# Block-count prefix of a token ranking: 31 TensorE products replaced by one VectorE scan of 512

## The chip, the cores and the metric

One Trainium2 chip, one of its cores. The metric is the device time of the whole program in microseconds (us), as a median over several executions. Lines are named L1, L2, ... after the line of the kernel before. The engines are PE (TensorE), DVE (VectorE), ACT (ScalarE), POOL (GpSimd) and SP (the DMA-issuing queue).

## The reference, cut to what matters

The input is layer-normalised and goes through two branches whose outputs are added to it: an attention with relative-position bias (16 heads, 4 x 512 tokens) and a block whose q, k, v and output maps are hard-routed binary trees of depth 8. Each of the 2048 tokens walks one tree down to one of 256 leaves and uses that leaf's own small two-layer network:

```python
def _fff(x, nw, nb, w1, b1, w2, b2, act):
    node = jnp.zeros(x.shape[:2], dtype=jnp.int32)
    for _ in range(DEPTH):
        logit = jnp.einsum('bsd,bsd->bs', x, nw[node]) + nb[node]
        node = 2 * node + 1 + (logit > 0).astype(jnp.int32)
    leaf = node - NN
    h = act(jnp.einsum('bsd,bsdl->bsl', x, w1[leaf]) + b1[leaf])
    return jnp.einsum('bsl,bsld->bsd', h, w2[leaf]) + b2[leaf]
```

There are four trees: q, k and v on the normalised input, and f on the attention's output.

## The kernel before, in words

Tokens stand as 16 tiles of 128 (NT = 16, P = 128). Eight neighbouring leaves make one block, so there are 32 blocks (BLK = 32). For each tree the kernel sorts the tokens by block: every token gets a slot in a padded list in which each block begins at a multiple of 128, POOL scatters the token rows to their slots in HBM, and the tree's network then runs on 48 tiles of the list in 12 groups of four, with one block's weights per tile.

The slot of a token is: the padded start of its block, plus the number of tokens of that block in earlier tiles, plus the number in earlier partitions of its own tile. `ranks` (L1023 to L1035, PE) and `ranked` (L613 to L638, DVE) compute it from a one-hot table `o` of 16 tiles x 32 blocks (512 columns, bf16).

- `ranks` waits for the one-hot (semaphore oh5). Into the PSUM bank rank[0] it puts one product with a strictly triangular matrix, which counts earlier partitions of the same tile (L1029), and 15 products with a matrix of ones: tile i's counts are broadcast over all later tiles, 480, 448, ... 32 columns wide (L1031). Into rank[1] it adds up 16 products of 32 columns, the total of every block (L1034). The last one raises rk.
- `ranked` waits for rk. It rounds the totals up to 128 (L618 to L620), makes a prefix over the 32 blocks by a scan (L622 to L625), adds it to rank[0] over 512 columns (L627, raises rt), multiplies by the one-hot and sums (L631, L632), writes the slots (L633, raises sl, for which POOL's scatter waits), and finds each list tile's block (L635 to L637, raises id). `then` makes an instruction raise a counter and DVE wait for it before the next one.

This runs four times. For q, k and v it lies in the opening stretch, one loop over 12 pieces i (three trees, four pieces each) on PE, DVE and ACT. On PE, piece i issues `logits(i)` (L994), at c = 2 `ranks` of the tree before, then `follow(i-1)` (L1005) and `settled(i-2)` (L1018). `settled` of a tree's first piece writes the banks that `ranked` reads, and so waits for rt. On DVE, piece i issues `bits_of(i)` (L645), at c = 1 `places` (L652 to L657, raises oh5), at c = 2 `ranked` to its end. ACT runs L845 on `follow`'s result, and later sends a small DMA per tree once id is raised (`tile_blocks`, L836).

After that PE does the v products (L1063), projections (`project`, L1070 to L1073) and the main loop: 16 steps of 20 slots, written out by hand. In a slot PE computes one 128 x 512 tile of scores twice (`scores_q`, L1084, for the row maximum, and `scores_k`, L1095 and L1097, for the exponential), DVE takes the maximum (`row_max`, L693), ACT the exponential (L873), and PE weighs values (L1107). `max_rows` (L1122) transposes the maxima after a step's last `row_max`, `sub_max` (L699) subtracts them, and the next step's `scores_k` waits for it. The stages of the trees' networks (L1155, L1161, L1166, L1171 on PE) are fitted into fixed slots.

The f tree's routing is fitted in too. `route_y` on PE issues `ranks` in slot 188. On DVE a generator, `route_f`, is advanced once per slot, behind that slot's `row_max`, from slot 174 on; each `yield` ends a slot's share. `ranked` falls into slots 196 (L618 to L620), 197 (L622 to L627) and 198 (L631 to L637); slot 199 is the last of its step. The f tree's network starts in slot 226.

Of the kernel before, what the change touches and what calls it, by code (L numbers as in the profile page):

```python
# [24 lines left out]
ALU = mybir.AluOpType  # L25
# [3 lines left out]
P = 128  # L29
NB, NS = 4, 512  # L30
KT = NS // P
NT = NB * KT
# [10 lines left out]
BLK = LEAVES // LB  # L43
# [73 lines left out]
def build(nc, x, wq, wk, wv, wp, bp, table, onehot, cf, cb, nw, nb, wl, b2, out):  # L117
# [7 lines left out]
    with ctx:  # L125
        def sb(name, shape, dt=F32):
            return ctx.enter_context(nc.sbuf_tensor(name, shape, dt))
# [50 lines left out]
        whole = sb("whole", [P, BLK], I32)  # L178
# [28 lines left out]
        ps = ctx.enter_context(nc.psum_tensor("ps", [P, 8, NS], F32))  # L207
# [5 lines left out]
        bank = lambda i: ps[:, i, :]  # L213

        S = {n: ctx.enter_context(nc.semaphore(n)) for n in (
            "d_ew0 d_ew1 d_ew2 d_ew3 d_x d_c d_w d_u d_b d_f d_z d_n d_sc tc pa oh hb pop z_mx pl tab_in d_far aug lkc mxc "
            "sl tick rt_in rt_out ones ln_m ln_r ln_sub ln_sq ln_out xT_ps xT_sb xnT_sb tab_ps tab_sb v_ps v_sb lg bit oh5 rk rt id wsc "
            "proj p1 mt p2 pv ot at pr h ex osb ats vr qs ks km max qs2 rc norm acc "
            "lx0 lx1 lw0 lw1 st xT xTs hh hr mk hm yy yl d_nf yT_ps yT_sb "
            "g_y g_v0 g_v1 g_v2 g_v3 g_b g_o0 g_o1 g_o2 g_o3 t_ps t_sb s_ps s_mx s_ex pT_ps pT_sb o_ps y_sb y_add dv d_out").split()}  # L220
# [261 lines left out]
        def _(dve):  # L482
            V = nc.vector
            count = [0]

            def then(ins):

                count[0] += 1
                ins.then_inc(S["dv"], 1)
                dve.wait_ge(S["dv"], count[0])  # L490
# [122 lines left out]
            def ranked(t, work, rank):  # L613

                here = work.bitcast(BF16)[:, 30 * NT:62 * NT].rearrange("p (t n) -> p t n", n=BLK)
                dve.wait_ge(S["rk"], t + 1)
                c = lambda i, n=BLK: sm[:, i, 0:n]
                then(V.tensor_scalar(whole[:], ps[:, rank[1], 0:BLK], float(P - 1), None, ALU.add))  # L618
                then(V.tensor_scalar(whole[:], whole[:], -P, None, ALU.bitwise_and))
                then(V.tensor_copy(c(0), whole[:]))  # L620
                yield
                V.memset(c(2), 1.0)  # L622
                then(V.memset(c(3), 0.0))
                then(V.tensor_tensor_scan(c(3), c(2), c(0), 0.0, ALU.mult, ALU.add))
                then(V.tensor_tensor(c(1), c(3), c(0), ALU.subtract))  # L625
                rows = work[:, 32 * NT:64 * NT].rearrange("p (t n) -> p t n", n=BLK)
                V.tensor_tensor(rows, bank(rank[0]).rearrange("p (t n) -> p t n", n=BLK),  # L627
                                c(1).unsqueeze(1).to_broadcast([P, NT, BLK]), ALU.add).then_inc(S["rt"], 1)
                dve.wait_ge(S["rt"], t + 1)
                yield  # L630
                then(V.tensor_tensor(rows, rows, here, ALU.mult))  # L631
                then(V.tensor_reduce(st[:, 5, :], rows, X, ALU.add))  # L632
                V.tensor_copy(slot[:, t, :], st[:, 5, :]).then_inc(S["sl"], 1)  # L633

                then(V.tensor_scalar(c(2), c(3), col(C_T), None, ALU.is_le))  # L635
                then(V.tensor_reduce(sm[:, 4, 0:1], c(2), X, ALU.add))
                then(V.tensor_scalar(ewc[:, t:t + 1], sm[:, 4, 0:1], float(BLK - 1), float(BLK * t), ALU.min, ALU.add))  # L637
                dve.sem_inc(S["id"], 1)  # L638
# [24 lines left out]
            for i in range(NTREE * CHUNKS + 3):  # L663
                if i < NTREE * CHUNKS:
                    bits_of(i)
                t, c = divmod(i, CHUNKS)
                if c == 1 and t > 0:
                    places(t - 1, t1)
                if c == 2 and t > 0:
                    for _ in ranked(t - 1, t1, (0, 1)):  # L670
                        pass
# [60 lines left out]
            def route_y():  # L732

                for k in range(4):
                    dve.wait_ge(S["yT_ps"], k + 1)
                    V.tensor_copy(yT[:, k * NS:(k + 1) * NS], bank(FB[k % 2])).then_inc(S["yT_sb"], 1)
                    if k % 2:
                        yield
                dve.wait_ge(S["d_nf"], 32)
                then(V.tensor_scalar(nb_f, nb_f, -1.0, None, ALU.mult))  # L740
                yield
                yield from decide(TF, nb_f, bits_f.bitcast(BF16)[:, 0:NT * NODES].rearrange("p (t n) -> p t n", n=NODES), work_f,
                                  [(k, FB[k % 2]) for k in range(8)])
                yield from ranked(TF, work_f, FB)
# [216 lines left out]
        def _(pe):  # L961
            T = nc.tensor
# [5 lines left out]
            for i, t in enumerate((xTs, hr)):  # L968
                b_ = WB - 1 + i
                last = T.matmul(ps[0:H, b_, :], tab_s, flat(t[0:BUCKETS]), start=True, stop=True)  # L970
# [52 lines left out]
            def ranks(t, work, rank):  # L1023

                wb = work.bitcast(BF16)
                o = wb[:, 30 * NT:62 * NT].rearrange("p (t n) -> p t n", n=BLK)
                tri, ones = cbt[:, 0], cbt[:, 1]
                pe.wait_ge(S["oh5"], t + 1)
                T.matmul(bank(rank[0]), tri, wb[:, 30 * NT:62 * NT], start=True, stop=False)  # L1029
                for i in range(NT - 1):  # L1030
                    T.matmul(ps[:, rank[0], (i + 1) * BLK:], ones, o[:, i:i + 1, :].to_broadcast([P, NT - 1 - i, BLK]),  # L1031
                             start=False, stop=i == NT - 2)
                for i in range(NT):
                    last = T.matmul(ps[:, rank[1], 0:BLK], ones, o[:, i, :], start=i == 0, stop=i == NT - 1)  # L1034
                last.then_inc(S["rk"], 1)  # L1035

            pe.wait_ge(S["xnT_sb"], 4)
# [3 lines left out]
            for h in range(2):  # L1041
                for k in range(2):
                    last = T.matmul(ps[:, PATH_BANKS[0], h:h + 1], paths[:, k, h * P:(h + 1) * P], cbt[:, 1, 0:1],
                                    start=k == 0, stop=k == 1)
            n = 2 * (NTREE + 1)
            T.transpose(ps[:, PATH_BANKS[0], 2:2 + n], nb_rows, cst[0:n, C_ID:C_ID + n]).then_inc(S["pop"], 1)
            pe.wait_ge(S["pop"], 2)
            for i in range(NTREE * CHUNKS + 3):
                if i < NTREE * CHUNKS:
                    logits(i)  # L1050
                t, c = divmod(i, CHUNKS)
                if c == 2 and t > 0:
                    ranks(t - 1, t1, (0, 1))
                if 1 <= i <= NTREE * CHUNKS:
                    follow(i - 1)
                if 2 <= i <= NTREE * CHUNKS + 1:
                    settled(i - 2)
# [3 lines left out]
            for k in range(4):  # L1061
                for i in range(4):
                    last = T.matmul(quarter(VB[k], i), xnT[:, (4 * k + i) * P:(4 * k + i + 1) * P], wv_s[:], start=True, stop=True)  # L1063
# [168 lines left out]
            def route_y(after):  # L1232

                for k in {0: (0, 1), 1: (2, 3)}.get(after, ()):
                    y_transposed(k)
                for k in {3: (0, 1), 4: (2,), 5: (3,), 6: (4,), 7: (5,), 8: (6,), 9: (7,)}.get(after, ()):
                    y_logits(k)
                if after == 14:
                    ranks(TF, work_f, FB)
# [130 lines left out]
```

## Time and profile before

| | us |
|---|---|
| median of 3 runs | 673.77 (671.25 to 674.9) |
| the profiled execution, its own time | 670.35 |
| its span in the trace | 668.3 |
| PE busy | 581.6 |
| DVE busy | 414.0 |
| ACT busy | 354.4 |
| POOL busy | 274.7 |

The profiled execution's own time is 2.05 us over its span, and 3.42 us under the median of the runs. Busy time counts instructions at work; idle time in brackets in a timeline is that of the engine just before the instruction, with what ended it. PEclk is the granted TensorE clock: 1.00 is 2.4 GHz, 0.50 is 1.2 GHz.

### The profile page before, as it was taken

What the parts mean: (1) busy time and instruction counts of PE and PEld (TensorE: products, weight loads), DVE (VectorE), ACT (ScalarE), POOL (GpSimd) and SP (SyncE); (2) the same over time, 40 slices, a digit from 0 to 9 for tenths busy, and PEclk for the clock granted to TensorE, in tenths of its full rate; (3) what the DMA queues carried; (4) which work ended last, traced back from release to release, by engine and by line L of the source; (5) the groups of instructions that cost most, each with busy time, mean ns of one, the idle gap of its engine ahead of it and who ended that gap; (6) DMA issues with size and microseconds to landing.
All of it is one profiled execution on the core that took longest, in us unless ns stands there. A gap on an engine that the chain in (4) does not pass through costs nothing.

```text
span 668.3 us, 11751 instructions
## 1 busy us (share of the span) xinstructions
PE 581.6 (87%) x3641; PEld 408.9 (61%) x3641; DVE 414.0 (62%) x967; ACT 354.4 (53%) x762; POOL 274.7 (41%) x288
## 2 busy tenths in 40 slices
PE   2289868999999999999999999988698989988976
PEld 0144457777777777777775656755265667675643
DVE  3856657666666666576766665576867564756730
ACT  4633323655556565555655546423244877786533
POOL 7951776770357870760038300000077800000880
PEclk9889998999999999999999999998789999999988
DMA  7988756785668794886512200000033654542231
GB/s 224 266 170 206 259 144 170 214 218 157 184 192 217 177 210 129 185 193 166 151 41 36 37 0 1 1 1 0 1 111 69 116 135 127 144 122 69 31 49 47
DMA packets 108701, 83.05 MB, mean 124 GB/s; under 512 B 8680, under 2 KB 105840, under 8 KB 108640
## 3 DMA queue, kind: packets, MB, share of 16 engines
q1 hardware_dynamic: 93344, 69.68, 38.8%
q0 software_dynamic: 15104, 12.63, 10.3%
q8 instruction: 29, 0.48, 0.3%
q14 instruction: 32, 0.26, 0.1%
q10 hardware_dynamic: 192, 0.00, 0.0%
HBM read 57.91 MB, written 24.36 MB: 123 GB/s over the span
## 4 chain that ended last, share of the span: by engine, by line
PE 62%; DVE 8%; ACT 8%; issue 5%; SPq 1%; DMA 0%; DVEq 0%; ACTq 0%
PE ps L1095 8%; PE ps L1107 8%; PE ps L1097 8%; PE ps L1084 7%; PE ps L1171 6%; PE ps L1161 6%; PE ps L1070 3%; DVE ps L693 3%; PE ps L1214 2%; PE ps L1228 2%; ACT hr L884 2%; ACT L873 2%; PE ps L1155 2%; PE ps L1166 2%; ACT L884 2%
## 5 line engine op out<-in xcount | busy, mean ns | idle before, releaser
L693 DVE CUSTOM_DVE_ANT_0 ps<-ps,strip 128x512 f32<-128x512 f32 x256 | 177.5, 699 | 110.9 <-PE ps L1084 105.2
L873 ACT ACTIVATE pt<-ps 128x512 f32<-128x512 f32 x256 | 150.6, 600 | 99.0 <-PE ps L1097 96.5
L1095 PE MATMUL ps<-qs,km 128*128 128x512 f32 x256 | 128.4, 501 | 8.7 <-ACT pt L873 7.4
L1084 PE MATMUL ps<-km,qs 128*128 128x512 f32 x256 | 112.1, 442 | 10.9 <-DVE mx L693 7.0
L432 POOL DMA_INDIRECT yt<-ys,slot x48 | 74.5, 1552 | 80.7 <-DMA ys<-yl 66.7
L884 ACT ACTIVATE hr<-ps,wt 128x128 f32<-128x128 f32 x192 | 54.9, 368 | 66.7 <-PE ps L1161 66.6
L1097 PE MATMUL ps<-u_lo,rev_r 128*128 128x220 f32 (+1 forms) x256 | 75.3, 294 | 0.0
L1097 PE MATMUL ps<-u_hi,rev_r 128*128 128x220 f32 (+1 forms) x256 | 73.8, 288 | 0.0
L1095 PEld LDWEIGHTS ps<-qs,km 128*128 128x128 f32 x256 | 49.6, 194 | 34.9 <-ACT pt L873 21.4
L427 POOL DMA_INDIRECT xs<-xr,slot x64 | 62.5, 977 | 19.7 <-issue 18.3
L1107 PE MATMUL ps<-pt,v_aug 128*32 128x512 f32 x512 | 69.9, 619 | 0.7 <-ACT pt L873 0.7
L425 POOL CAST xr<-part_of 128x16 f32<-128x16 int32 x4 | 0.9, 213 | 156.9 <-DVE slot L633 130.4
L1161 PEld LDWEIGHTS ps<-xTs,wt 128*128 128x128 f32 x384 | 48.3, 194 | 24.6 <-issue 21.7
L1084 PEld LDWEIGHTS ps<-km,qs 128*128 128x128 f32 x256 | 49.5, 194 | 21.7 <-DVE mx L693 13.8
L432 POOL DMA_INDIRECT xr<-ys,slot x16 | 25.1, 1571 | 86.9 <-DMA ys<-yl 82.4
L1097 PEld LDWEIGHTS ps<-u_lo,rev_r 128*128 128x128 f32 x256 | 49.1, 192 | 11.4
L1161 PE MATMUL ps<-xTs,wt 128*128 128x128 f32 x384 | 54.5, 286 | 1.7 <-DMA wt<-in_wl 1.7
L432 POOL DMA_INDIRECT yt<-in_b,leaf x48 | 45.8, 954 | 20.6 <-issue 14.0
L1097 PEld LDWEIGHTS ps<-u_hi,rev_r 128*128 128x128 f32 x256 | 50.0, 195 | 5.1 <-issue 4.1
L1171 PE MATMUL ps<-wt,hm 128*128 128x128 f32 x384 | 52.4, 280 | 0.7
L1171 PEld LDWEIGHTS ps<-wt,hm 128*128 128x128 f32 x384 | 49.8, 194 | 4.5 <-DVE hm L725 3.1
L725 DVE SCALAR_TENSOR_TENSOR hm<-ps,cst,hr 128x512 f32<-128x512 f32 x48 | 36.0, 749 | 17.7 <-ACT hr L884 11.5
(227 smaller groups left out, 898.0 us busy)
## 6 DMA issues: line engine op xcount, KB each, us to landing
wt<-in_wl SPq DMA_DIRECT2D x192, 128.5 KB, 2.3
xl<-xs SPq DMA_DIRECT2D x48, 258.0 KB, 3.6
ys<-yl SPq DMA_DIRECT2D x48, 256.0 KB
xs<-mx SPq DMA_DIRECT2D x2, 3096.0 KB, 21.6
strip<-bias_bf SPq DMA_DIRECT2D x1, 3584.0 KB, 37.1
u_hi<-bias_hi SPq DMA_DIRECT2D x1, 2496.0 KB, 15.7
u_lo<-bias_lo SPq DMA_DIRECT2D x1, 2496.0 KB, 28.1
xs<-xr,slot POOLq DMA_INDIRECT x64
```

The source lines that it names most:

```text
L427: pool.indirect_dma_start(out=xs[t % 2][:, :], out_offset=bass.IndirectOffsetOnAxis(ap=slot[:, t, k:k + 1], axis=0), in_=xr[:, k, :], in_o ...
L432: pool.indirect_dma_start(out=dst, out_offset=None, in_=src[:, :], in_offset=bass.IndirectOffsetOnAxis(ap=idx, axis=0), compute_op=op).the ...
L693: V.tensor_tensor_reduce(out=bank(u % 2), in0=bank(u % 2), in1=strip[:, HG * g + j, b0:b0 + NS], scale=1.0, scalar=LOWEST, op0=ALU.add, op ...
L725: V.scalar_tensor_tensor(flat(hm[:]), bank(BB[k]), col(C_LEAF), flat(hr[:]), ALU.is_equal, ALU.mult).then_inc(S["hm"], 1)
L873: A.activation(pt[:, kt % 2, j, :], bank(2 + u % 2), ACT.Exp).then_inc(S["ex"], 1)
L884: last = A.activation(hr[:, i, :], ps[:, BB[k], i * P:(i + 1) * P], ACT.Relu if n < NTREE * GROUPS else ACT.Gelu, bias=wt[:, par, i, 2 * P ...
L1084: T.matmul(bank(u % 2), qs[:, par, qt * P:(qt + 1) * P], backward(km[:, par, j, :]), start=True, stop=True).then_inc(S["p1"], 1)
L1095: T.matmul(bank(2 + u % 2), km[:, par, j, kt * P:(kt + 1) * P], qs[:, par, :], start=True, stop=False)
L1097: last = T.matmul(ps[:, 2 + u % 2, lo:hi], rev_r[:], half[:, HG * g + j, u0:u0 + hi - lo], start=False, stop=stop)
L1107: last = T.matmul(ps[HR * j:HR * j + HR, OB, :], v_aug[:, par, kt, j, :], pt[:, kt % 2, j, :], start=kt == 0, stop=kt == KT - 1)
L1161: last = T.matmul(quarter(BB[k], i), wt[:, par, i, 0:P], xTs[:, i, :], start=True, stop=True)
L1171: last = T.matmul(quarter(BB[k], i), hm[:, i, :], wt[:, par, i, P:2 * P], start=True, stop=True)
```

## The change

`ranks` keeps the triangular product and replaces the 15 + 16 others by one product with the matrix of ones over all 512 columns, read block by block (moving operand with tiles innermost), so that rank[1] holds every tile's count of every block, ordered block, tile. `ranked` makes one running sum over these 512 counts, into `run` (513 columns of `work`, the first of them zero). The difference of the sums at a block's end and its beginning is the block's total; the running sum before a tile, less the sum at the block's beginning, is the number of tokens in earlier tiles. So `c(1)` is lessened by the sums at the blocks' beginnings, and `rows` takes a second addition of 512 columns, of `starts`, read with the two axes exchanged. A `yield` is added between the two additions, and rt is raised by the second. One memset (of `c(3)`) goes, one (of the first column of `run`) comes, and `whole` is made from `c(0)` in SBUF.

```diff
-                then(V.tensor_scalar(whole[:], ps[:, rank[1], 0:BLK], float(P - 1), None, ALU.add))
+                run = work[:, 64 * NT:96 * NT + 1]
+                starts = run[:, 0:32 * NT].rearrange("p (n t) -> p n t", t=NT)
+                V.memset(run[:, 0:1], 0.0)
+                then(V.memset(c(2), 1.0))
+                then(V.tensor_tensor_scan(run[:, 1:32 * NT + 1], c(2)[:, 0:1].to_broadcast([P, 32 * NT]),
+                                          bank(rank[1]), 0.0, ALU.mult, ALU.add))
+                then(V.tensor_tensor(c(0), run[:, 1:32 * NT + 1].rearrange("p (n t) -> p n t", t=NT)[:, :, NT - 1], starts[:, :, 0],
+                                     ALU.subtract))
+                then(V.tensor_scalar(whole[:], c(0), float(P - 1), None, ALU.add))
                 then(V.tensor_scalar(whole[:], whole[:], -P, None, ALU.bitwise_and))
                 then(V.tensor_copy(c(0), whole[:]))
                 yield
-                V.memset(c(2), 1.0)
-                then(V.memset(c(3), 0.0))
                 then(V.tensor_tensor_scan(c(3), c(2), c(0), 0.0, ALU.mult, ALU.add))
                 then(V.tensor_tensor(c(1), c(3), c(0), ALU.subtract))
+                then(V.tensor_tensor(c(1), c(1), starts[:, :, 0], ALU.subtract))
                 rows = work[:, 32 * NT:64 * NT].rearrange("p (t n) -> p t n", n=BLK)
-                V.tensor_tensor(rows, bank(rank[0]).rearrange("p (t n) -> p t n", n=BLK),
-                                c(1).unsqueeze(1).to_broadcast([P, NT, BLK]), ALU.add).then_inc(S["rt"], 1)
+                then(V.tensor_tensor(rows, bank(rank[0]).rearrange("p (t n) -> p t n", n=BLK),
+                                     c(1).unsqueeze(1).to_broadcast([P, NT, BLK]), ALU.add))
+                yield
+                V.tensor_tensor(rows, rows, starts.rearrange("p n t -> p t n"), ALU.add).then_inc(S["rt"], 1)
                 dve.wait_ge(S["rt"], t + 1)
...
             def ranks(t, work, rank):
 
                 wb = work.bitcast(BF16)
-                o = wb[:, 30 * NT:62 * NT].rearrange("p (t n) -> p t n", n=BLK)
                 tri, ones = cbt[:, 0], cbt[:, 1]
                 pe.wait_ge(S["oh5"], t + 1)
-                T.matmul(bank(rank[0]), tri, wb[:, 30 * NT:62 * NT], start=True, stop=False)
-                for i in range(NT - 1):
-                    T.matmul(ps[:, rank[0], (i + 1) * BLK:], ones, o[:, i:i + 1, :].to_broadcast([P, NT - 1 - i, BLK]),
-                             start=False, stop=i == NT - 2)
-                for i in range(NT):
-                    last = T.matmul(ps[:, rank[1], 0:BLK], ones, o[:, i, :], start=i == 0, stop=i == NT - 1)
+                T.matmul(bank(rank[0]), tri, wb[:, 30 * NT:62 * NT], start=True, stop=True)
+                by_block = wb[:, 30 * NT:62 * NT].rearrange("p (t n) -> p n t", n=BLK)
+                last = T.matmul(bank(rank[1]), ones, by_block, start=True, stop=True)
                 last.then_inc(S["rk"], 1)
```

## Rows read from the trace of the kernel before

**Rows 1.** The page, part 4: shares of the chain that ended last.

```profile
PE 62%; DVE 8%; ACT 8%; issue 5%; SPq 1%; DMA 0%; DVEq 0%; ACTq 0%
```

**Rows 2.** Busy time by stretches: from:to, length, busy by engine, PEclk, DMA share, GB/s.

```profile
64.70:72.70 8.00, 8.00 (x48) 3.86 (x47) 5.43 (x10) 3.80 (x6) 6.18 (x7) 1.00 0.99 363
```

**Rows 3.** Timeline, first ranking: start, length, engine, line, operation, count, idle before.

```profile
57.39 1.43 DVE L645 TENSOR_SCALAR yt<-ps,nbT 128x512 bf16<-128x512 f32 x2
...
57.87 0.38 PE L1029 MATMUL ps<-pt,cbt 128*128 128x512 bf16 x1
...
58.09 1.80 PE L1031 MATMUL ps<-pt,cbt 128*128 128x480 bf16 x15
...
60.14 1.02 PE L1005 MATMUL ps<-yt,b_pT 128*128 128x512 bf16 x4
60.33 0.19 DVE L618 TENSOR_SCALAR whole<-ps 128x32 int32<-128x32 f32 x1 [1.50 <-PE ps L1034]
...
61.44 0.19 DVE L625 TENSOR_TENSOR sm<-sm 128x32 f32<-128x32 f32 x1
61.67 0.69 DVE L627 TENSOR_TENSOR pt<-ps,sm 128x512 f32<-128x512 f32 x1
...
62.51 0.35 PE L1018 MATMUL ps<-b_pT,yt 128*128 128x33 bf16 x8 [1.35 <-DVE pt L627]
...
64.72 1.41 DVE L645 TENSOR_SCALAR yt<-ps,nbT 128x512 bf16<-128x512 f32 x2
```

**Rows 4.** Timeline, third ranking and the start of the main loop.

```profile
87.57 0.19 DVE L618 TENSOR_SCALAR whole<-ps 128x32 int32<-128x32 f32 x1 [2.34 <-PE ps L1034]
...
91.16 1.28 ACTq L836 DMA_DIRECT2D ew<-ewc  x2
...
91.80 1.12 PE L1070 MATMUL ps<-xnT,wk_s 128*128 128x512 f32 x2 [0.69 <-ACT v_all L849]
...
93.32 0.60 ACT L861 ACTIVATE ks<-ps 128x512 fp32r<-128x512 f32 x1 [1.57 <-PE ps L1073]
...
97.34 0.80 PE L1084 MATMUL ps<-km,qs 128*128 128x512 f32 x1 [3.34 <-DVE qs L676]
```

**Rows 5.** Timeline, the f tree's ranking in the main loop and after it.

```profile
461.01 0.39 PE L1029 MATMUL ps<-yt,cbt 128*128 128x512 bf16 x1 [2.06 <-DVEq L591]
...
463.95 0.77 PE L1095 MATMUL ps<-qs,km 128*128 128x512 f32 x1
...
465.85 0.70 DVE L693 CUSTOM_DVE_ANT_0 ps<-ps,strip 128x512 f32<-128x512 f32 x1 [3.15 <-PE ps L1084]
...
482.73 0.69 DVE L631 TENSOR_TENSOR yt<-yt 128x512 f32<-128x512 f32 x1
...
485.20 0.70 DVE L693 CUSTOM_DVE_ANT_0 ps<-ps,strip 128x512 f32<-128x512 f32 x1 [0.30 <-DVE ewc L637]
...
486.01 1.06 PE L1122 MATMUL ps<-cst,mx 128*128 128x128 f32 x4 [3.40 <-DVE mx L693]
...
487.11 0.69 DVE L699 TENSOR_TENSOR qs<-qs,ps 128x512 fp32r<-128x512 f32 x1 [1.16 <-PE ps L1122]
...
488.65 0.99 PE L1095 MATMUL ps<-qs,km 128*128 128x512 f32 x1
...
506.69 16.72 SPq L266 DMA_DIRECT2D xl<-xs  x3
...
518.77 0.66 PE L1155 MATMUL ps<-cst,xl 128*128 128x128 f32 x4
```

**Rows 6.** Groups by form on DVE: line, shapes, count, busy us, mean ns, idle.

```profile
L631 DVE TENSOR_TENSOR pt<-pt 128x512 f32<-128x512 f32 x3 | 2.1, 692 | 0.1
...
L624 DVE TENSOR_TENSOR_SCAN sm<-sm 128x32 f32<-128x32 f32 x4 | 0.9, 225 | 0.1
```

**Rows 7.** Busy time in two stretches at the lower clock (columns as in Rows 2).

```profile
462.40:465.40 3.00, 3.00 (x30) 2.68 (x29) 0.30 (x1) 0.12 (x1) 0.00 (x0) 0.50 0.00 0
97.00:103.60 6.60, 6.26 (x23) 5.17 (x24) 3.57 (x10) 1.74 (x5) 5.02 (x6) 0.50 0.29 89
```

## Prediction, made before the changed kernel was run

> **What bounds the kernel now.** I read the chain that ended last first: TensorE holds 62% of it and VectorE 8% [rows 1], so on the whole an instruction saved on PE is worth something and one added on DVE little. But the ranking lies at four places, and each has a bound of its own, so the timelines decide. In the opening stretch PE and DVE take turns around a ranking: DVE finishes `bits_of` at 58.82 (57.39 + 1.43), idles 1.50 us until PE's products are done, works from 60.33 without a break to its next `bits_of` at 64.72, and PE in turn idles 1.35 us until `ranked` has read the banks, at 62.51 [rows 3]. So the ranking is a closed path, PE then DVE then PE. Behind it PE has no gap: 8.00 busy of 8.00 us [rows 2], so a late start of `settled` is not caught up. The second ranking repeats this. The third differs: no `bits_of` follows. In the main loop PE waits 2.06 us for the one-hot, computes `ranks` from 461.01 to 463.95, and DVE's `row_max` waits 3.15 us for it; later it is turned round, and PE's `max_rows` waits 3.40 us for DVE [rows 5].
>
> **Rankings one and two.** PE: the triangular product runs 0.38 us and the next starts 0.22 behind it [rows 3]. The one new product, the same 512 columns at the same pace, ends near 58.09 + 0.38 = 58.5, instead of 60.3 for the last of the 31. DVE is free only at 58.82, so it starts 60.33 - 58.85 = 1.48 us sooner. DVE gets longer by:
> - the scan of 512. 512 elements of an ordinary operation take 0.692 and 32 take 0.19 [rows 6, 3]: 1.04 ns each over 0.16 fixed. The scan of 32 takes 0.225, so its elements cost (0.225 - 0.16) / 32 = 2.0 ns: 512 take 0.16 + 1.05 = 1.2 us. Bounds: 0.69 (one element a cycle, the 32-element excess being fixed) and 1.2; I take 1.2, which the row for the scan itself gives.
> - two subtractions of 32, 0.19 each, and one addition of 512, 0.69 [rows 3]; each of the four dependent instructions also costs the 0.04 that stands between L625's end at 61.63 and L627 at 61.67.
> - the memsets: two before, two after, nothing. `whole` from SBUF instead of PSUM: nothing that matters.
>
> Sum 1.2 + 0.38 + 0.69 + 0.16 = 2.43, less 1.48: **+0.95 each**, 1.9 for both. It lies on the path twice over, in rt (PE's `settled`) and in DVE's next `bits_of`. Queued behind the later rt on PE are the next `logits`, `follow` and `settled`, and ACT waits for those. POOL's first scatter starts 0.95 later with sl; its rows are wanted far later than they come, and the main loop moves by as much.
>
> **Ranking three.** PE's 1.8 us sooner end moves the v products forward. The projection at 91.80 waited for ACT's copies of them [rows 4] and would come sooner, but then waits for rt. DVE starts 1.8 sooner (it idled 2.34) and works 2.43 longer: +0.6. That delays id, and with it ACT's second small DMA, which ended at 92.44 (91.16 + 1.28) and now ends near 93.1. ACT's L861, next on that queue, started at 93.32 [rows 4]. So the 0.6 is just covered and PE's gain cannot pass ACT: **0**, between -0.2 and +0.4.
>
> **The clock in the opening.** Here is the cost that no instruction shows. After the change PE ends `ranks` at 58.5 and `follow` (1.02 long [rows 3]) near 59.4, and then has nothing until `settled` at 62.51 + 0.95 = 63.5: 4.1 us of idling instead of 1.35. In this trace an idle of 2.06 us and one of 3.34 us [rows 5, 4] were each followed by the 1.2 GHz level, some 3 us after the idling began, for 3.0 us and for 6.6 us [rows 7]; the 1.35 us were not. A fall near 62.5 that lasts 3.0 us covers 2.0 us of PE-bound work at half speed and loses 1.0; one of 6.6 us loses 2.8. I take 1.3, near the shorter, since PE is full right behind the wait. After ranking two little `logits` work is left and DVE and ACT share the path: 0.3 to 2.3, I take 0.6. Together **+1.9**; lower bound 0, if the clock holds.
>
> **Ranking four.** PE: `ranks` took 2.94 us (461.01 to 463.95); two products take 0.22 + 0.22 + about 0.2 of change-over, 0.65. PE is on the path there, so the scores and DVE's `row_max` at 465.85 come 2.3 sooner; DVE, 3.15 idle, has room for it [rows 5]. From there DVE sets the pace to the end of the step. The added `yield` moves the rest, L631 to L637, from slot 198 to slot 199, behind the last `row_max`. So before `max_rows` DVE gains 485.20 - 482.73 = 2.47 and pays 2.43 + 0.30 for one more hand-over between a slot's share and the next `row_max` (the 0.30 before 485.20): +0.3. `max_rows` starts 2.3 - 0.3 = 2.0 sooner, at 484.0. Then the moved rest stands in front of `sub_max` on DVE: 2.2 us against the 1.06 us of transposes it can hide behind [rows 5]. `sub_max` starts near 486.2 and ends near 486.9, so `scores_k`, at 488.65 before, comes at 486.9: **-1.8** (bounds -2.9, all that PE saves, and -0.5, if PE runs at half clock between the longer DVE stretches). The rest also raises sl and id some 0.8 later: POOL's 16 scatters and SP's small DMA follow them, and SP's load of the first rows, at 506.69, is issued 0.8 later in the trace's time; its first use is at 518.77 [rows 5], so 12 us cover it, less the 1.8 by which that use comes sooner.
>
> **Sum:** 1.9 + 0 + 1.9 - 1.8 = +2.0 us, 0.3%. The profiled execution was 670.35 us, 3.42 below the median, and would become 672.4; on the median of 673.77 that is **675.8**. A measurement of this kernel can tell about 0.5%, 3.4 us, from no change, so this is no measurable change.
>
> **A rule against the change.** No row here has an engine read SBUF in steps of 64 bytes, as the new product's moving operand, the two subtractions and the second addition do. By bounds from the nearest rows an addition of 512 lies between 0.69 (contiguous) and twice that. The Trainium skill, SBUF — State Buffer, section on the DMA port swizzle, says that SBUF has lines of 16 bytes and that each access that crosses to a new line pays a penalty. By that rule every element here would pay, and the time would be that of rival 2; the sum above has none of it.
>
> **Rivals.**
> 1. *The clock holds.* For it: other short waits of PE left it at 2.4 GHz. Against: 2.06 us were enough once. Sum +0.1: 673.9. Chance 0.25.
> 2. *Slower: the strided reads run at half rate.* Place: the second addition (+0.53, once per ranking, on the path in one, two and four, and 0.3 in three), and the new product (+0.22; hidden behind `bits_of` in one and two, on the path in four, where 0.4 with the lower clock). 3 x 0.53 + 0.3 + 0.4 = +2.3 on top of 2.0: 678.1. It decides once these cost 1.4 us together, about 1.6 times the contiguous rate. Nothing in the trace speaks for or against it. Chance 0.2.
> 3. *Faster: the opening's delay is swallowed by the first weight loads and all 2.9 us of ranking four are kept, the clock held.* Price -2.9: 670.9, and with the runs' own spread beyond -3.4. Against: SP's weight loads are issued when PE's stages free the buffers, so they move along. Chance 0.08.
>
> **How the numbers follow.** Forecast 0.47, the rivals 0.25, 0.2 and 0.08. The range runs from 671.0 (rival 3; rival 1 with a scan at one element a cycle, 1.5 less, is inside) to 679.5 (rival 2 with part of the longer low-clock stretch). Slower by over 0.5%: most of rival 2, and a third of the forecast, since its two clock terms may be 3 us larger: 0.29. Faster by over 0.5%: 0.06. Within: 0.65.
>
> **What would show it.** In the changed profile: L1031 and L1034 gone and one 512-column product in their place; a scan of 512 at 1.2 us; DVE busy from about 58.9 to 65.7 around the first ranking; PE idle about 4 us there with the granted clock at 0.50 behind it; `row_max` after the fourth ranking without its 3.15 us wait; the rest of `ranked` behind the step's last `row_max`. The forecast is wrong if the second addition takes over 1 us, if the clock stays at 1.00 to 72 us, or if the main loop's start moves by other than 2 to 5 us.

## The result, and the profile after

The changed kernel takes **681.53 us** (median of 6 runs, 679.81 to 685.15) beside 672.75 us for the kernel before (6 runs): a ratio of 1.0126, interval 1.0081 to 1.0172. That is 8.8 us slower by the medians and 8.5 by the ratio; 681.53 lies above the end of the range at 679.5. The profiled execution took 685.15 us, with a span of 683.1. Of its 14.8 us over the profile before, 4.2 had already passed ahead of the first ranking, where the code is the same (e3 below, with the old opening, also gets there 3.5 us later than that profile, and e11 3.7); so everything below is measured from one event to another within an execution.

The timeline of the changed kernel around the first ranking, answering to [rows 3]: L661 is `places`' conversion, L1037 and L1039 the two products, L622 the new scan, L634 and L637 the two additions, L1027 `settled`, L1003 `logits`.

```profile
60.48 0.69 DVE L661 CAST pt<-ps 128x512 bf16<-128x512 f32 x1 [0.30 <-PE ps L1027]
...
62.09 0.38 PE L1037 MATMUL ps<-pt,cbt 128*128 128x512 bf16 x1
62.31 1.02 PE L1039 MATMUL ps<-pt,cbt 128*128 128x512 bf16 x1
...
63.40 0.06 DVE L620 MEMSET pt<- 128x1 f32 x1 [0.35 <-PE ps L1039]
...
63.53 1.22 DVE L622 TENSOR_TENSOR_SCAN pt<-sm,ps 128x512 f32<-128x512 f32 x1
...
66.41 0.69 DVE L634 TENSOR_TENSOR pt<-ps,sm 128x512 f32<-128x512 f32 x1
67.14 1.02 DVE L637 TENSOR_TENSOR pt<-pt 128x512 f32<-128x512 f32 x1
...
68.30 0.39 PE L1027 MATMUL ps<-b_pT,yt 128*128 128x33 bf16 x8 [4.11 <-DVE pt L637]
68.53 3.76 PE L1003 MATMUL ps<-yt,v_all 128*128 128x512 f32 x4
```

The new product takes 1.02 us where its neighbour with the same 512 columns takes 0.38, and DVE idles 0.35 us for it. The scan is as long as forecast, the second addition half as long again. PE waits 4.11 us, and the four products behind it take 3.76 us; four such products take 1.96 us at 57.43 in the same trace. Why shows in the windows (columns as in [rows 2]):

```profile
64.00:67.70 3.70, 0.19 (x1) 0.00 (x0) 3.39 (x10) 1.07 (x2) 0.00 (x0) 0.97 1.03 199
67.70:74.10 6.40, 5.80 (x25) 2.48 (x25) 4.00 (x9) 0.75 (x2) 3.30 (x4) 0.50 1.05 391
...
88.00:91.80 3.80, 3.75 (x13) 1.60 (x14) 2.66 (x8) 0.00 (x0) 2.51 (x3) 0.56 0.14 48
```

Behind the first wait PE works at the 1.2 GHz level for some 6.8 us (67.5 to 74.3), behind the second for 3.4 (87.9 to 91.3; the rest of that window, at 1.00, lifts its mean to 0.56), and is busy nearly all of that. The third ranking and the start of the main loop, answering to [rows 4] (L845 sends the blocks' indices by ACT's queue, L870 is ACT's next work):

```profile
98.34 1.22 DVE L622 TENSOR_TENSOR_SCAN pt<-sm,ps 128x512 f32<-128x512 f32 x1
...
103.28 2.75 ACTq L845 DMA_DIRECT2D ew<-ewc  x2
...
105.28 0.15 DVE L646 TENSOR_SCALAR ewc<-sm 128x1 int32<-128x1 f32 x1
106.21 0.60 ACT L870 ACTIVATE ks<-ps 128x512 fp32r<-128x512 f32 x1 [2.34 <-PE ps L1075]
...
110.19 0.80 PE L1089 MATMUL ps<-km,qs 128*128 128x512 f32 x1 [4.07 <-DVE qs L685]
```

ACT's copy now starts where the index DMA ends (103.28 + 2.75 = 106.03): the DMA that [rows 4] show ended 0.88 us ahead of the copy has come onto the path. The copy starts 0.78 us behind the end of L646, at which id is raised; it does so in e1, e4, e13 and e14 too, while before it came 1.48 us behind. The ranking of the f tree, answering to [rows 5] (the record of its L1037 is missing; the product starts some 0.2 us ahead of L1039):

```profile
476.38 1.02 PE L1039 MATMUL ps<-yt,cbt 128*128 128x512 bf16 x1 [2.29 <-DVEq L591]
...
478.95 0.70 DVE L702 CUSTOM_DVE_ANT_0 ps<-ps,strip 128x512 f32<-128x512 f32 x1 [1.11 <-PE ps L1089]
...
497.56 1.01 DVE L637 TENSOR_TENSOR yt<-yt 128x512 f32<-128x512 f32 x1
...
499.41 0.69 DVE L640 TENSOR_TENSOR yt<-yt 128x512 f32<-128x512 f32 x1
499.61 1.12 PE L1127 MATMUL ps<-cst,mx 128*128 128x128 f32 x4 [3.31 <-DVE mx L702]
...
501.73 0.69 DVE L708 TENSOR_TENSOR qs<-qs,ps 128x512 fp32r<-128x512 f32 x1
...
502.47 0.81 PE L1100 MATMUL ps<-qs,km 128*128 128x512 f32 x1
```

`row_max` waits 1.11 us in place of 3.15, and the moved rest (from L640 on) stands ahead of `sub_max` (L708), as forecast. Groups by form, answering to [rows 6] (count, busy us, mean ns):

```profile
L622 DVE TENSOR_TENSOR_SCAN pt<-sm,ps 128x512 f32<-128x512 f32 x3 | 3.7, 1222 | 0.1
L637 DVE TENSOR_TENSOR pt<-pt 128x512 f32<-128x512 f32 x3 | 3.1, 1027 | 0.1
...
L624 DVE TENSOR_TENSOR sm<-pt 128x32 f32<-128x32 f32 x3 | 0.6, 212 | 0.1
```

### The profile page after: what moved, and what is told of

Same layout as the page of the kernel before. It is cut to its first block, busy times and chain, and to the rows that moved or that the text cites. A ratio compares the mean times of both kernels' runs of the same rounds, so it can differ in the third digit from the quotient of the medians.

```text
span 683.1 us, 11506 instructions
## 1 busy us (share of the span) xinstructions
PE 585.4 (86%) x3500; PEld 409.4 (60%) x3521; DVE 430.3 (63%) x983; ACT 354.3 (52%) x762; POOL 274.0 (40%) x288
## 4 chain that ended last, share of the span: by engine, by line
PE 61%; DVE 8%; ACT 7%; issue 4%; another core or an unknown queue 2%; DMA 1%; SPq 1%; DVEq 0%; ACTq 0%
PE ps L1100 8%; PE ps L1112 8%; PE ps L1102 8%; PE ps L1089 7%; PE ps L1166 6%; PE ps L1176 6%; PE ps L1075 3%; PE ps L1160 2%; PE ps L1171 2%; PE ps L1219 2%; PE ps L1233 2%; DVE ps L702 2%; ACT L882 2%; ACT hr L893 2%
## 5 line engine op out<-in xcount | busy, mean ns | idle before, releaser
L893 ACT ACTIVATE hr<-ps,wt 128x128 f32<-128x128 f32 x192 | 54.7, 368 | 68.0 <-PE ps L1166 67.9
L1166 PEld LDWEIGHTS ps<-xTs,wt 128*128 128x128 f32 x384 | 49.8, 199 | 25.4 <-issue 21.8
```

The source lines that it names most:

```text
L893: last = A.activation(hr[:, i, :], ps[:, BB[k], i * P:(i + 1) * P], ACT.Relu if n < NTREE * GROUPS else ACT.Gelu, bias=wt[:, par, i, 2 * P ...
L1166: last = T.matmul(quarter(BB[k], i), wt[:, par, i, 0:P], xTs[:, i, :], start=True, stop=True)
```

## The experiments

Line numbers of the experiments' rows are their own; the tiles and the order are those above. Two tables serve all of them. The first follows the opening, in us, in each kernel's profiled execution: "conv" is `places`' conversion on DVE (L652 before), "settled" the group of products that waits for rt (L1018), "scores" the first `scores_q` (L1084). So a column ending at "settled" is the ranking's path through PE and DVE, and a column beginning there is what PE and DVE do behind it.

| kernel | conv 1 to settled | settled to conv 2 | conv 2 to settled | settled to conv 3 | conv 3 to scores | sum |
|---|---|---|---|---|---|---|
| before | 6.25 | 8.99 | 6.24 | 6.40 | 13.20 | 41.08 |
| after | 7.82 | 11.78 | 7.82 | 8.01 | 14.28 | 49.71 |
| e1 | 7.82 | 10.41 | 7.82 | 8.79 | 14.03 | 48.87 |
| e2 | 7.82 | 10.49 | 7.87 | 8.80 | 14.04 | 49.02 |
| e3 | 6.24 | 8.99 | 6.24 | 6.40 | 13.22 | 41.09 |
| e4 | 7.73 | 9.00 | 7.73 | 6.41 | 14.05 | 44.92 |
| e5 | 8.62 | 10.99 | 9.03 | 8.63 | 15.48 | 52.75 |
| e6 | 8.42 | 10.68 | 8.42 | 8.91 | 15.99 | 52.42 |
| e9 | 6.25 | 8.99 | 6.23 | 6.40 | 15.78 | 43.65 |
| e10 | 6.24 | 9.00 | 6.24 | 6.40 | 14.63 | 42.51 |
| e11 | 6.24 | 8.99 | 6.24 | 6.40 | 13.22 | 41.09 |
| e12 | 6.25 | 8.99 | 6.24 | 6.40 | 13.24 | 41.12 |
| e13 | 7.34 | 9.00 | 7.52 | 6.41 | 14.60 | 44.87 |
| e14 | 7.33 | 9.00 | 7.54 | 6.41 | 13.61 | 43.89 |

The last column needs care. In e9 and e10, whose opening is that of before, it is 2.6 and 1.4 us longer: in these executions the granted clock is 0.50 from 88.5 to 95.3 us and from 88.3 to 91.7, during ranking three, though no wait of PE in the 20 us ahead of it was longer than 1.35 us. In before, e3, e11 and e12 the same instructions run at 1.00 there. So this column tells of the change only where the clock is alike; e1 and e2, at 1.00 from 92 to 108 us, are fit for that.

The second follows the f tree's ranking, from the first product of `ranks`:

| kernel | to `max_rows` | to the next `scores_k` |
|---|---|---|
| before | 25.00 | 27.64 |
| after | 23.4 | 26.3 |
| e3 (f only) | 23.43 | 26.28 |
| e5 (old arithmetic for f) | 23.62 | 26.30 |
| e11 (before, idle products) | 23.62 | 25.15 |
| e10 (f only, idle products) | 22.83 | 25.69 |
| e12, e14 (product turned round, idle products) | 22.54 | 25.40 |

**Which rankings lose: e1, e2 and e3.** e1 is the changed kernel once more. e2 keeps the old `ranks` and `ranked` for the f tree, e3 for q, k and v.

```diff
 e2: the changed kernel, with the functions of before as ranks_f and ranked_f
-                    yield from ranked(TF, work_f, FB)
+                    yield from ranked_f(TF, work_f, FB)
...
-                    ranks(TF, work_f, FB)
+                    ranks_f(TF, work_f, FB)
 e3: the same two calls in the kernel before, ranks_f and ranked_f being the changed functions
```

> The changed kernel once more, for a second profile beside the first. Both theories: a ratio to before of 1.008 to 1.017. Theory A (the loss lies in the opening: about 3.1 us of longer VectorE path in rankings one and two and 4.4 us of TensorE at 1.2 GHz behind their waits, less 1.4 us gained in ranking four): from the start of bits_of before the first ranking to the first L1089 about 48.6 us, against 40.0 in the profile of before, and the part of the 14.8 us between the two profiles that lies ahead of the first ranking (4.2 us) and in the main loop (about 3 us) shrinks, as spread between executions. Theory B (a good part of the loss is in the main loop, from the changed program as such): those two parts stay.

> The change for the q, k and v rankings only; the f ranking as before. Theory A: before + 8.5 us (ratio about 1.0125), 1.4 us slower than the whole change. Theory B: before + 4 to 5, clearly faster than the whole change, as the main loop's part is gone.

> The change for the f ranking only; q, k and v as before. Theory A: 1.4 us faster than before (ratio 0.998), the opening's times those of before. Theory B: 2 to 4 us slower than before.

Measured: e1 1.0066 (1.0027 to 1.0104), e2 1.0113 (1.0047 to 1.0179), e3 0.9995 (0.996 to 1.003). The loss is in the opening: e3's opening is that of before to 0.02 us, e2's is 7.9 us longer (1.2%). In both e1 and e2 a ranking's path is some 1.6 us longer, twice, what follows it 3.8 to 3.9 us longer in sum, and the third part 0.8. Ranking four gives 1.4 us back in e3 (27.64 to 26.28), too little for its ratio to show. From the tables e1 should lose 7.8 less 1.1 (its ranking four ends 26.5 us behind its start), 6.7 us, and the first runs 8.6 less 1.3, 7.3 us; both lie where the two intervals overlap (5.4 to 7.0 us) or 0.3 us beyond. Theory B of e1, a loss in the main loop, has nothing for it: from the first `scores_q` to the end of the span e1 takes 570.1 us, before 571.0. The part ahead of the first ranking did not shrink in e1 as theory A expected (its conversion is at 60.40), but it differs as much among kernels with the old opening (56.26 to 60.78).

**The clock: e4 and e6.** e4 keeps PE busy through the waits of the opening. The products' result is not used: the next `logits` overwrites the bank. e6 is the kernel before with its addition of 512 done four times instead of once, so rt comes later and PE waits longer, with PE's own work unchanged.

```diff
 e4, in settled(i), ahead of the wait for rt
+                    pe.wait_ge(S["bit"], 2 * (i + 3) - 2)
+                    for _ in range(16):
+                        T.matmul(bank(LOGIT_BANKS[(i + 3) % 2][0]), cbt[:, 1], t1.bitcast(BF16)[:, 30 * NT:62 * NT],
+                                 start=True, stop=True)
 e6, in ranked, ahead of the addition that raises rt
+                if t < TF:
+                    for _ in range(3):
+                        then(V.tensor_tensor(rows, bank(rank[0]).rearrange("p (t n) -> p t n", n=BLK),
+                                             c(1).unsqueeze(1).to_broadcast([P, NT, BLK]), ALU.add))
```

> The whole change, and 16 products of 512 columns into a free PSUM bank while TensorE waits for rt in rankings one and two; their result is overwritten, nothing else differs. Theory A: the granted clock stays 1.00 behind both waits and the opening is 4.4 us shorter than in the changed kernel: ratio to before about 1.006. Rival C (the clock is low there, but VectorE and ScalarE set the pace, so it costs nothing): the clock stays up and the time stays at 1.0126.

> The kernel before, with one addition of rankings one to three done four times over, so that rt comes 2.2 us later; TensorE's work is the same as before. Theory A: TensorE's idle before settled grows from 1.35 to about 3.5 us, its clock falls behind it, and the opening grows by 4.4 us of VectorE path and 2 to 4 us more of slow clock: 6.5 to 8.5 us, ratio about 1.010 to 1.0125. Rival C (no cost by the clock): 4.4 us, ratio 1.0065, granted clock 1.00.

Measured: e4 1.0037 (1.0006 to 1.0068). Its PE timeline behind the first wait, and its windows behind both:

```profile
63.39 3.62 PE L1025 MATMUL ps<-pt,cbt 128*128 128x512 bf16 x16
67.58 0.37 PE L1031 MATMUL ps<-b_pT,yt 128*128 128x33 bf16 x8 [0.57 <-DVE pt L637]
67.80 1.96 PE L1003 MATMUL ps<-yt,v_all 128*128 128x512 f32 x4
```

```profile
67.00:74.00 7.00, 6.43 (x42) 3.19 (x42) 5.47 (x11) 2.17 (x4) 3.53 (x5) 1.00 1.05 390
84.00:91.00 7.00, 4.81 (x44) 2.54 (x44) 3.98 (x10) 2.53 (x4) 4.93 (x5) 1.00 0.17 57
```

With the products in the gap the clock stays at 1.00, `logits` takes 1.96 us again, and both columns behind `settled` are those of before (9.00 and 6.41), while the columns of the path keep their loss. So the 3.8 to 4.4 us are the clock's, and the clock fell because PE stood idle. What is left of e4's opening over that of before, 3.84 us, less the 1.2 that its ranking four gains, makes 2.7 us, the 0.4% measured. e6 came out at 1.0168 (1.0098 to 1.0238), more than expected: its PE waits 3.52 us, and here too the clock falls, in the old arithmetic.

```profile
68.09 0.35 PE L1022 MATMUL ps<-b_pT,yt 128*128 128x33 bf16 x8 [3.52 <-DVE pt L631]
68.29 2.96 PE L998 MATMUL ps<-yt,v_all 128*128 128x512 f32 x4
```

```profile
67.00:74.00 7.00, 5.91 (x27) 2.65 (x28) 4.46 (x11) 1.37 (x2) 3.39 (x4) 0.76 1.06 384
```

A delay of 2.2 us per ranking on DVE cost 11.3 us in e6's opening (52.42 less 41.08): 4.3 on the two paths, 4.2 behind them, 2.8 at the third. The lower clock lasts from 69.1 to 72.5 us and, behind the second wait, from 86.2 to 93.0. In all, PE waits 3.5 to 5.1 us for rt ten times in the profiles of after, e1, e2, e5 and e6, and the clock falls at each; the lengths of the low stretches, 3.4 or some 6.8 us, do not follow the lengths of the waits: behind 4.11 and 4.11 us the first profile has 6.8 and 3.4, e1 has 3.4 (67.9 to 71.3) and 6.9 (84.9 to 91.8).

**The strides: e5 and e13.** e5 stores the one-hot of rankings one to three block by block, so both products and both additions read contiguously; its ranking four is that of before, so e2 is the kernel to compare it with. e13 is e4 with the new product turned round: it reads contiguously and writes PSUM in steps of 64 bytes, with the same result.

```diff
 e5, in places: the conversion writes the one-hot with tiles innermost
-                V.tensor_copy(work.bitcast(BF16)[:, 30 * NT:62 * NT].rearrange("p (a t n) -> p a t n", a=2, n=BLK),
+                V.tensor_copy(work.bitcast(BF16)[:, 30 * NT:62 * NT].rearrange("p (n a t) -> p a t n", a=2, n=BLK),
 e5, in ranks and ranked: the reads follow that order; ranking four keeps the functions of before
 e13, in ranks
-                by_block = wb[:, 30 * NT:62 * NT].rearrange("p (t n) -> p n t", n=BLK)
-                last = T.matmul(bank(rank[1]), ones, by_block, start=True, stop=True)
+                by_tile = wb[:, 30 * NT:62 * NT].rearrange("p (t n) -> p t n", n=BLK)
+                last = T.matmul(bank(rank[1]).rearrange("p (n t) -> p t n", t=NT), ones, by_tile, start=True, stop=True)
```

> Rankings one to three of the changed kernel with the one-hot stored block by block, so that both products and both 512-column additions read contiguously; the f ranking as before. The transposed steps move to the write of the one-hot (ahead of the ranking) and to the last reduction (behind rt). Compared with the opening-only kernel. Theory A: the product of the tile counts 0.38 instead of 1.02 long, the second addition 0.69 instead of 1.02, so PE's wait for rt is about 0.4 to 0.7 us shorter in rt's time (7.8 from the cast to settled becomes about 7.1), but TensorE still idles 3.8 us and falls to 1.2 GHz: ratio to before about 1.009. Rival D (the strided reads are what made the forecast fail): most of the loss goes, ratio below 1.004.

> The whole change with the 16 idle products behind the waits of the opening, and the new product turned round everywhere: it reads its 512 columns one after another and writes PSUM in steps of 64 bytes. Theory A (DVE's idle of 0.35 us ahead of the scan is the slow reading of that product, and lies on the path of rankings one and two): the idle goes, the time from the first to the third conversion of places (30.87 us with the idle products and the reading in steps) falls by 0.6 to 0.8, and the ratio is about 1.0025. Rival (the 0.35 us only takes the place of another wait, for follow or bits_of): the time between the conversions stays within 0.2 us of 30.87.

e5 measured 1.0165 (1.01 to 1.023), beside 1.0113 for e2: the expected gain did not come. Its timeline:

```profile
59.53 2.32 DVE L688 CAST pt<-ps 128x512 bf16<-128x512 f32 x1 [0.30 <-PE ps L1054]
...
62.20 0.38 PE L1065 MATMUL ps<-pt,cbt 128*128 128x512 bf16 x1
...
67.31 0.69 DVE L637 TENSOR_TENSOR pt<-pt 128x512 f32<-128x512 f32 x1
...
68.15 0.39 PE L1054 MATMUL ps<-b_pT,yt 128*128 128x33 bf16 x8 [4.71 <-DVE pt L637]
...
68.76 1.01 DVE L641 TENSOR_REDUCE st<-pt 128x16 f32<-128x512 f32 x1
```

The product is back at 0.38 and the second addition at 0.69, which shows that the layout alone made them slow. But the conversion, which now writes bf16 in steps of 32 bytes, takes 2.32 us in place of 0.69, and stands ahead of the products. PE's waits grew to 4.71 and 5.12 us. e13 measured 1.0011 (0.998 to 1.0042):

```profile
61.71 0.59 PE L1043 MATMUL ps<-pt,cbt 128*128 128x512 bf16 x1
```

```profile
62.53 1.22 DVE L622 TENSOR_TENSOR_SCAN pt<-sm,ps 128x512 f32<-128x512 f32 x1
```

The product takes 0.59 us. The scan starts 2.65 us behind the conversion, in e4 3.04 (62.89 less 59.85), and from the first conversion to the third pass 30.27 us in place of 30.87: the 0.35 us of idling were on the path, as theory A said (0.60 us, the low end of what it expected). The last column lost it again here (14.60), at a clock of 0.50 from 90 to 97 us; e14, with the same product and the clock at 1.00, has 13.61.

**Ranking four and the start of the main loop: e9 to e12 and e14.** These put idle products, whose result is overwritten, at the other places where the clock fell. e9 is the kernel before with 14 at the start of the main loop. e10 is e3 with those and with more ahead of ranking four and through it, e11 the kernel before with all of e10's, e12 is e10 with the product with ones turned round (its expectation calls it the tri product; the triangular one is left as it was). e14 is the whole change with the product turned round and idle products at all places.

```diff
 e9 to e12, e14: behind project(0, 0, 0, 0)
+            for _ in range(14):
+                T.matmul(bank(2), cbt[:, 1], kr[:], start=True, stop=True)
 e10 to e12, e14: ahead of ranking four, and in the slots behind it
+                    pe.wait_ge(S["bit"], 8 * TF + 8)
+                    for _ in range(8):
+                        T.matmul(bank(FB[0]), cbt[:, 1], kr[:], start=True, stop=True)
...
+                    if 191 <= slot_of(n, at) <= 199 and at < SLOTS - 1:
+                        pe.wait_ge(S["norm"], n)
+                        for _ in range(6 if at >= 15 else 3):
+                            T.matmul(bank(WB), cbt[:, 1], kr[:], start=True, stop=True)
```

> The kernel before, with 14 products of 512 columns into a free bank while TensorE waits 3.3 us for the first scores of the main loop. Theory A (an idle of TensorE of 2 us or more is paid for behind it): the 6.6 us at 1.2 GHz that followed are gone and 2 to 3 us with them, ratio about 0.996. Rival C: VectorE and SP set the pace there, no difference.

> The change for the f ranking only, the same 14 products at the start of the main loop, 8 while TensorE waits for the f tree's one-hot and 3 to 6 per slot in the slots in which VectorE sets the pace (191 to 198). Theory A: 1.5 us from the ranking, 2 to 3 from the start, 1 to 2 from the step's end, where max_rows and the projections ran at 1.2 GHz: ratio 0.991 to 0.994. Rival C: only the 1.5 us, ratio 0.998.

> The kernel before with all the extra idle products of the previous run (at the start of the main loop, ahead of ranking four and through it), and none of the change. Theory A (the change in ranking four is worth about 1.4 us by itself, and the idle products the rest of that run's gain): ratio 0.996 to 0.997, 1.4 to 2 us slower than the previous run. Rival (the idle products are all of its gain and the change in ranking four gives nothing): equal to the previous run, 0.994.

> The f-only change with all the idle products, and the tri product of ranking four alone turned round: it reads its 512 columns one after another and writes them to PSUM in steps of 64 bytes, so that the scan and the additions see the same layout as before. Theory A (it is the reading of the moving operand in steps that takes 0.85 instead of 0.22 us): the product falls from 1.02 to about 0.4 us, and the kernel is some 0.3 to 0.6 us faster than the one that reads in steps, a ratio of about 0.993 to 0.994. Rival (a step of 64 bytes costs the same on the side of PSUM): the product stays at 1.0 us or more, and the ratio is that of the one that reads in steps.

> The whole change with the product turned round and idle products at all places (behind the two waits of the opening, at the start of the main loop, ahead of ranking four and through it). Theory A (with the clock held, the change costs VectorE's longer path in the opening, some 2.4 us, and the third ranking, some 0.8, and earns 1.8 in ranking four, so that it is 1 to 2 us slower than the kernel before with the same idle products, whose ratio was 0.998): 0.999 to 1.001. Rival (what is left of the opening's loss is swallowed before the main loop, and ranking four decides): 0.995 to 0.997, as the f-only kernels.

| kernel | median, us | before beside it, us | ratio and interval |
|---|---|---|---|
| e9 | 674.15 | 675.71 | 0.9975 (0.9943 to 1.0007) |
| e10 | 671.62 | 675.71 | 0.9944 (0.9909 to 0.9978) |
| e11 | 672.22 | 673.28 | 0.998 (0.9949 to 1.0011) |
| e12 | 671.75 | 673.28 | 0.9974 (0.9944 to 1.0004) |
| e14 | 673.74 | 675.15 | 0.9966 (0.9939 to 0.9993) |

By their intervals e10 and e14 are faster than the kernel before. The change is not shown to be the cause: e11, without it, overlaps both, and ran beside e12 with medians 0.5 us apart. e10 and e12 have medians 0.1 us apart, and most of the difference between their ratios is that of the runs beside them. e9 leaves both its theories open; in its trace the first step of the main loop, from the first `scores_q` to `max_rows`, takes 21.02 us in place of 22.14, with the clock at 1.00 from 96 to 122 us. e11's ratio alone lies nearer to its theory A (0.996 to 0.997) than to the rival's 0.994. The trace says more than the ratios. e11, around its ranking four:

```profile
464.74 0.39 PE L1029 MATMUL ps<-yt,cbt 128*128 128x512 bf16 x1 [0.33 <-DVEq L591]
464.97 1.80 PE L1031 MATMUL ps<-yt,cbt 128*128 128x480 bf16 x15
...
468.20 0.70 DVE L693 CUSTOM_DVE_ANT_0 ps<-ps,strip 128x512 f32<-128x512 f32 x1 [1.77 <-PE ps L1084]
...
488.36 0.65 PE L1122 MATMUL ps<-cst,mx 128*128 128x128 f32 x4 [3.52 <-DVE mx L693]
...
489.89 0.99 PE L1095 MATMUL ps<-qs,km 128*128 128x512 f32 x1
```

The 15 products take 1.80 us, where [rows 7] had them at the lower clock, and `row_max` waits 1.77 us in place of 3.15. The old arithmetic then needs 25.15 us to `scores_k`, the changed one 25.40 to 25.69. So theory A of e11 fell and its rival's mechanism holds: with the clock held, ranking four gains nothing from the change. It reaches `max_rows` 0.8 to 1.1 us sooner and loses 1.3 to the rest that was moved ahead of `sub_max` (2.86 us from `max_rows` to `scores_k`, in e11 1.53). The 1.4 us that the change gave here were time at the lower clock. e5 shows the same without idle products: its ranking four has the old arithmetic and PE's wait of 2.06 us, but in that execution the clock stayed at 1.00 from 469 to 491 us; the 15 products take 1.80 us, and `scores_k` comes after 26.30 us, where the changed kernels need 26.3 to 26.5. In e12 the product takes 0.59 us in place of 1.02 (between theory A's 0.4 and the rival's 1.0) and `scores_k` comes 0.29 us sooner than in e10; the ratios can't tell these apart.

e14 was expected 1 to 2 us behind e11. Its opening is 2.8 us longer and its ranking four 0.25; its first step of the main loop, from the first `scores_q` to `max_rows`, is 1.15 us shorter than e11's (19.62 to 20.77). The sum of these, 1.9 us, is what its one profiled execution takes over e11's (spans of 671.5 and 669.6 us). The ratio lies in the rival's range, but its interval reaches theory A's, and it can't be told from e11's: each of the two intervals is some 4 us wide, and 2 us do not show in them.

## Why the prediction was wrong

- **Rankings one and two, +0.95 each: the term was mis-sized, 1.57 measured.** The scan (1.22, forecast 1.2) and the small operations (0.21, forecast 0.19) were right. "The one new product, the same 512 columns at the same pace" was wrong: it takes 1.02 us, so DVE idles 0.35 where it should have found the product done. The second addition takes 1.02, not 0.69. Together 0.68 more, nearly the 0.62 missing. e5 shows that both come from the layout, e13 that the idling lay on the path.
- **Rival 2 had the place and not the prices.** It gave the product +0.22 and hid it in rankings one and two; it was +0.64 and not hidden. It gave the second addition +0.53; it was +0.33. The Trainium skill, SBUF — State Buffer, section on the DMA port swizzle, which the prediction named for lines of 16 bytes with a penalty for each line crossed, agrees with the sign of both rows. The same passage of the Trainium skill says that PSUM's lines are of 8 bytes and that patterns that are not contiguous there slow matmuls; e13's 0.59 us beside 0.38 agrees.
- **The clock in the opening, +1.9: mis-sized, 3.8 to 4.4 measured, and the largest miss.** The wait was forecast at 4.1 us and is 4.11; that close an agreement is luck, as the slow product ends PE's work 0.6 us later and rt is 0.6 us later too. But the low stretch was taken near 3.0 us, from the row behind a 2.06 us idle, with 0.6 us for ranking two because little `logits` work is left there. In the first profile it lasted some 6.8 and 3.4 us, with PE busy 6.0 and 3.4 of them; half of that, 3.0 and 1.7, is close to what the two columns lost (2.79 and 1.61). In e1 PE was busy 3.1 and 5.4 us at the lower clock, and the columns lost 1.42 and 2.39. So the longer stretch of [rows 7], priced at 2.8 us, came once in each, and nothing in the wait's length says where.
- **Ranking three, 0: failed, +0.8 to +1.1.** The step that failed is "So the 0.6 is just covered". DVE starts 1.15 us sooner, not 1.8, and works 2.7 to 3.0 us longer, not 2.43 (the slow product and the second addition again), so id comes 1.6 us later behind the conversion in e1 and 1.8 in the first profile. The cover was there, 0.70 us (1.48 less 0.78), and too short: 1.57 less 0.70 is 0.87 in e1, where the column lost 0.83, and 1.82 less 0.70 is 1.12 in the first profile, where it lost 1.08. The index DMA then holds ACT's copy, the place that the prediction named.
- **Ranking four, -1.8: right in sign and place, -1.1 to -1.4.** `row_max`'s 3.15 us went to 1.11, and it came 2.0 us sooner behind the first product (e3) where 2.3 were forecast, as the new product is slow here too; the rest moved ahead of `sub_max`. What the prediction did not see is that the whole gain was the lower clock's (e11, e5).
- **Sum.** Forecast 1.9 + 0 + 1.9 - 1.8 = 2.0; by e1's terms 3.15 + 0.83 + 3.81 - 1.14 = 6.65. Rival 2's slow reads and the longer low stretch, which the prediction priced apart, came together. Two of its three signs of being wrong are there: the second addition takes over 1 us, and the main loop's start moves by 8.6 us (7.8 in e1). Rival 1, that the clock holds, was false here; e4 makes its condition, and is still 0.4% slower.

## What to carry to other kernels

Before a wait on a busy engine is lengthened, price what PE does behind it at half its pace, once for the shortest and once for the longest low stretch that the traces show: here one and the same wait was followed by either. A gain elsewhere may itself be time at the lower clock, and goes once the clock is held. Work that replaces many small products by one must be costed with its access pattern: a transposed read is paid by whoever reads it, and turning it into a transposed write can be cheaper (PSUM, 0.59 us) or far dearer (DVE in bf16, 2.32 us). Idle products in a known gap keep the clock, as e4 shows, but do not shorten the path that made the gap.

## What the runs showed of the hardware that was not expected

- A bf16 moving operand read from SBUF in steps of 64 bytes: 1.02 us for 512 columns, 0.38 contiguous. Less the 0.16 us between the 0.38 and the 0.22 at which the next product follows [rows 3], that is by estimate 0.86 to 0.22, four times. At the granted clock of 0.50 it takes 1.04 us (e1 and e4, ranking four) where its contiguous neighbour takes 0.60, so the time of the read in steps is hardly the clock's. Written to PSUM in steps of 64 bytes instead: 0.59 us.
- On DVE an f32 addition of 512 with one operand in steps of 64 bytes takes 1.02 us in place of 0.69, a reduction 1.01 in place of 0.69; a bf16 write in steps of 32 bytes 2.32 in place of 0.69.
- Waits of 3.52 to 5.12 us on PE in the opening (after, e1, e2, e5, e6, two each) all brought the lower clock, and 1.4 to 2.8 us of loss behind them; with 16 products of 0.22 us in the wait (e4, both waits) it stayed at 1.00. A short wait is no warrant either way: 2.06 us ahead of ranking four brought the lower clock to the kernel before and not to e5, and in e9 and e10 it fell in ranking three behind waits of at most 1.35 us.
